# A decoder layer: the second norm's shift added in PSUM, its centring shared by VectorE, TensorE, ScalarE and GpSimd

## What is computed

```python
x = layernorm(x + self_attention(x))
x = layernorm(x + cross_attention(x, ctx))
# feed-forward part
h = gelu(silu(bitlinear158(x, w1, b1)))          # 256 -> 1024
h = (h - mean(h)) * rsqrt(var(h) + eps) * ln_g + ln_b   # "the second norm"
y = bitlinear158(h, w2, b2)                      # 1024 -> 256
x = layernorm(x + y)

def bitlinear158(x, w, b):      # 8-bit numbers times weights of -1, 0, 1
    r = x * rsqrt(mean(x * x) + eps)
    scale = 127 / max(abs(r))
    return (round(r * scale) / scale) @ quantised(w).T + b
```

## Time and profile before

| | us |
|---|---|
| median of 3 runs (lowest, highest) | 528.34 (527.87, 529.71) |
| the profiled execution | 528.22 |
| its span in the trace | 525.7 |
| busy in the span: PE / DVE / ACT / POOL | 427.8 / 439.2 / 370.2 / 294.2 |
| the tail, from its first gelu to the span's end | 421.0 to 525.7 |

### The profile page before, as it was taken

How to read it: one execution, slowest core, us unless ns; L and a number is a source line. 1 busy time by engine, 2 the same in 40 slices (tenths; PEclk the granted TensorE clock), 3 DMA queues, 4 the chain that set the end, 5 groups by cost and what they waited for, 6 DMA issues and landing times. The chain is left out here.

```text
span 525.7 us, 11922 instructions
## 1 busy us (share of the span) xinstructions
PE 427.8 (81%) x4130; PEld 231.0 (44%) x4138; DVE 439.2 (84%) x942; ACT 370.2 (70%) x690; POOL 294.2 (56%) x407
## 2 busy tenths in 40 slices
PE   6777899999999999999999999998996602555554
PEld 5453545555555555554545545443432101333332
DVE  2857697988979889799998998988877769999993
ACT  2232366778678786777877767677769878999983
POOL 6744566446474464745557455577232157667653
PEclk9998799999999999999999999999999855555557
DMA  6122313243252422424234232221000000000001
GB/s 222 50 78 65 108 42 112 67 137 113 68 153 66 138 75 65 148 56 139 76 95 144 57 109 63 68 83 52 3 2 0 1 0 1 21 21 20 32 31 40
DMA packets 52459, 37.05 MB, mean 70 GB/s; under 512 B 21552, under 2 KB 47792, under 8 KB 52400
## 3 DMA queue, kind: packets, MB, share of 16 engines
q1 hardware_dynamic: 52112, 36.06, 23.8%
q10 hardware_dynamic: 288, 0.23, 0.2%
HBM read 24.48 MB, written 10.49 MB: 67 GB/s over the span
## 5 line engine op out<-in xcount | busy, mean ns | idle before, releaser
L886 ACT ACTIVATE PB<-e_b 128x512 f32<-128x512 f32 x256 | 148.2, 592 | 59.1 <-PE e_b L683 58.0
L1080 DVE TENSOR_REDUCE MX<-mx_b 128x2 f32<-128x512 f32 x256 | 166.7, 678 | 25.3 <-PE mx_b L655 24.0
L655 PE MATMUL mx_b<-KA,QA 48*128 48x256 bf16 x512 | 98.1, 277 | 11.1 <-DVE MX L1080 10.7
L683 PE MATMUL e_b<-QA,KA 50*128 50x256 bf16 x512 | 97.3, 274 | 0.7 <-ACT PB L886 0.5
L700 PE MATMUL u_b<-PB,VA 128*32 128x256 f32 x1024 | 84.0, 391 | 2.0 <-ACT PB L886 1.7
L1007 POOL TENSOR_TENSOR SP<-SP,srec 128x1024 f32<-128x1024 f32 x15 | 28.5, 1901 | 77.7 <-DVE srec L1052 77.7
L655 PEld LDWEIGHTS mx_b<-KA,QA 48*128 48x128 bf16 x512 | 29.9, 94 | 86.0 <-issue 46.8
L1420 PE MATMUL r_b<-identh,Q 128*128 128x128 f16 x128 | 16.2, 306 | 39.4 <-ACT Q L1333 39.4
L1426 PE MATMUL z_b<-w2q,Q2T 128*128 128x256 bf16 x128 | 28.5, 400 | 19.3 <-ACT Q2T L1344 19.3
L997 POOL TENSOR_TENSOR KM<-QK,att_tab 128x512 f32<-128x512 f32 x31 | 32.0, 1053 | 21.2 <-ACT QK L840 21.2
L560 PE MATMUL g_b<-XT,wp 128*128 128x128 f32 x256 | 34.5, 291 | 4.5 <-DMA wp<-in_wpT 4.5
(11 more groups left out here) (190 smaller groups left out, 1027.2 us busy)
## 6 DMA issues: line engine op xcount, KB each, us to landing
KA<-parts_k SPq DMA_DIRECT2D x64, 96.0 KB
QA<-parts_q SPq DMA_DIRECT2D x64, 96.0 KB
parts_q<-part_q SPq DMA_DIRECT2D x32, 128.0 KB, 1.9
parts_k<-part_k SPq DMA_DIRECT2D x16, 192.0 KB, 2.1
C<-in_ctx SPq DMA_DIRECT2D x16, 128.0 KB, 3.4
X<-in_x SPq DMA_DIRECT2D x16, 128.0 KB, 2.9
out_y<-O SPq DMA_DIRECT2D x16, 128.0 KB, 1.7
XT<-in_xT SPq DMA_DIRECT2D x15, 128.0 KB, 2.2
```

The costliest lines, as they stand in the source:

```text
L655: m = nc.tensor.matmul(mx_b[n % 2][:, D * k:D * k + D], QA[low:low + K_MAX, 2 * i.ring + b, h, P * u:P * u + P], KA[low:low + K_MAX, 2 * i ...
L683: m = nc.tensor.matmul(e_b[n % 2][:, D * k:D * k + D], KA[low:low + K_EXP, 2 * i.ring + b, h, P * sc:P * sc + P], QA[low:low + K_EXP, 2 * ...
L886: nc.scalar.activation(PB[:, n % 4].rearrange("p e t -> p (e t)"), e_b[n % 2][:, :], ACT.Exp, scale=XC ** -0.5).then_inc(e_sb.sem, 1)
L1080: nc.vector.tensor_reduce(MX[:, b, e, 2 * q:2 * q + 2, u], mx_b[n % 2][:, :].rearrange("p (e s) -> p e s", e=2), AXL.X, ALU.max).then_inc( ...
```

## The change

It touches the tail and, for tables that the tail needs, three bodies of phase A.

1. Beta is added in PSUM. In bodies 10, 11 and 12 POOL splits beta into three bf16 parts (`row_parts`, ten small steps into BP, and a selector `sel`). For each pair PE writes beta with two bf16 matmuls of 512 columns, 96 rows deep, into one of three two-bank buffers `n_b` (`row_sum`), and adds the rows to it in the same buffer (`row_product`). DVE's add of beta (L1459) is gone.
2. The centring is divided. Of the columns 0 to 383 (SPLIT) DVE takes the mean off and multiplies by gamma in one instruction (`lower_columns`); the scale comes from PE, whose stationary matrix is a diagonal `DG` that holds each row's root, made by POOL. Columns 384 to 1023 go the old way, ACT (L1323) and POOL (L1371), now 640 columns wide, and PE adds them with the identity as stationary matrix. Both products are fp32. The last pair's rows are all 1024 columns of DVE's and the diagonal's.
3. The maximum (DVE), the squares and the numbers (ACT) read n_b in PSUM in place of the rows in SBUF. The numbers' and the copy's constants are immediates of a Copy (they were pointers of an Identity).
4. The additions of eps (three small DVE instructions, `base`) are one POOL instruction ahead of the power.
5. All of it has a turn less of lag from the norm on: squares at 4 (the maximum at 3), numbers at 5, result at 6; 24 turns. r_b and z_b have one buffer each. PE has a list by turns: `row_sum` of pair t-3, product of pair t-6, `row_product` of pair t-3, transposes of pair t-5.

The diff, cut:

```diff
+            def row_parts(steps):
+                for k in steps:
+                    if k > 0:
+                        pool.wait_ge(s_bp, k)
...
+                    elif k == 4:
+                        pool.wait_ge(ld_rows, 16 * 4)
+                        ins = nc.gpsimd.tensor_copy(BP[own], bet[own])
+                    elif k == 5:
+                        ins = nc.gpsimd.tensor_tensor(BR[own], bet[own], BP[own], ALU.subtract)
+                    elif k == 6:
+                        ins = nc.gpsimd.tensor_copy(BP[mid], BR[mid])
+                    elif k == 7:
+                        ins = nc.gpsimd.tensor_copy(BP[low], BR[low])
+                    elif k == 8:
+                        ins = nc.gpsimd.tensor_tensor(BR[low], BR[low], BP[low], ALU.subtract)
+                    else:
+                        ins = nc.gpsimd.tensor_copy(BP[low], BR[low])
+                    ins.then_inc(s_bp, 1)
+                pool.wait_ge(s_bp, steps.stop)
...
+                if i.v in (10, 11, 12):
+                    wait(pool, split["q"], j, 5)
+                    row_parts((range(0, 5), range(5, 8), range(8, 10))[i.v - 10])
                 if real(a):
                     self_norm(pool, nc.gpsimd, a)
...
-        r_b = [bank(f"r_b{n}", F16) for n in range(2)]
-        z_b = [bank(f"z_b{n}") for n in range(2)]
+        tail_banks.close()
+        n_b = [es.enter_context(nc.psum_tensor(f"n_b{n}", [P, INNER], F32)) for n in range(3)]
+        r_b, z_b = bank("r_b", F16), bank("z_b")
-        TURNS2 = NPAIR + 9
+        TURNS2 = NPAIR + 8
...
-        LAG_G, LAG_N, LAG_Z = 1, 5, 7
+        LAG_G, LAG_N, LAG_Z = 1, 4, 6
...
-                if i := pair_at(t, 3):
+                if i := pair_at(t, 4):
+
+                    wait(act, ymax, i, 1)
+                    if has(i, 1):
+                        wait(act, sqr, i.plus(-1), 1)
+                    nc.scalar.activation(SQ[:], n_b[i.ring][:, :], ACT.Square, scale=INNER ** -0.5,
+                                         accum_out=mom[:, t % 2, 3:4]).then_inc(sqr.sem, 1)
+                j = pair_at(t, 5)
+                if j:
+                    wait(act, fac, j, 3)
+                    if has(j, 2):
+                        wait(act, q2_ps, j.plus(-2), 1)
+                    nc.scalar.activation(Q2[:, j.p, :], n_b[j.ring][:, :], ACT.Copy, bias=ROUND16,
+                                         scale=sc[:, j.v, 6:7]).then_inc(qd.sem, 1)
+                if (i := pair_at(t, 2)) and i.v != NPAIR - 1:
                     wait(act, shift, i, 1)
-                    nc.scalar.activation(row_h(i), row_h(i), ACT.Identity, bias=nmh[:, i.p, 0:1],
+                    nc.scalar.activation(row_h(i)[:, SPLIT:], row_h(i)[:, SPLIT:], ACT.Identity, bias=nmh[:, i.p, 0:1],
                                          scale=root[:, (i.v + LAG_G) % 4, 0:1]).then_inc(zs.sem, 1)
                 if i := pair_at(t, 0):
                     wait(act, silu, i, 1)
                     nc.scalar.activation(row_h(i), row_h(i), ACT.Gelu).then_inc(gelu.sem, 1)
-                j = pair_at(t, 6)
-                if j:
-                    wait(act, fac, j, 3)
-                    if has(j, 2):
-                        wait(act, q2_ps, j.plus(-2), 1)
-                    nc.scalar.activation(Q2[:, j.p, :], row_h(j), ACT.Identity, bias=rnd16[:],
-                                         scale=sc[:, j.v, 6:7]).then_inc(qd.sem, 1)
-                if i := pair_at(t, 4):
-                    wait(act, yn, i, 1)
-                    if has(i, 1):
-                        wait(act, sqr, i.plus(-1), 1)
-                    nc.scalar.activation(SQ[:], row_h(i), ACT.Square, accum_out=sc[:, i.v, 0:1]).then_inc(sqr.sem, 1)
                 if j:
                     wait(act, q2_ps, j, 1)
                     if has(j, 2):
                         wait(act, z_ps, j.plus(-2), 1)
-                    nc.scalar.activation(Q2T[:, j.p].rearrange("p k t -> p (k t)"), r_b[j.p][:, :],
-                                         ACT.Identity, bias=nrnd16[:]).then_inc(q2_sb.sem, 1)
+                    nc.scalar.activation(Q2T[:, j.p].rearrange("p k t -> p (k t)"), r_b[:, :],
+                                         ACT.Copy, bias=-OFF16).then_inc(q2_sb.sem, 1)
 
...
+            def power(t, cols, lags):
+                if not any(pair_at(t, lag) for lag in lags):
+                    pool.sem_inc(s_root, 1)
+                    return
+                if LAG_G in lags and (i := pair_at(t, LAG_G)):
+                    wait(pool, hn, i, 3)
+                if LAG_N in lags and (i := pair_at(t, LAG_N)):
+                    wait(pool, sqr, i, 1)
+                if LAG_Z in lags and (i := pair_at(t, LAG_Z)):
+                    wait(pool, zn, i, 3)
+                nc.gpsimd.tensor_tensor(base[:, t % 2, cols], mom[:, t % 2, 1::2][:, cols], eps3[:, cols], ALU.add).then_inc(s_eps, 1)
+                powers.append(t)
+                pool.wait_ge(s_eps, len(powers))
+                nc.gpsimd.tensor_tensor(root[:, t % 4, cols], base[:, t % 2, cols], halves[:, cols], ALU.pow).then_inc(s_root, 1)
+
             def turn(t):
-                if i := pair_at(t, 4):
-
-                    wait(pool, yn, i, 1)
-                if (i := pair_at(t, 3)) and i.v != NPAIR - 1:
-                    wait(pool, zs, i, 1)
-                    nc.gpsimd.tensor_tensor(row_h(i), row_h(i), gam, ALU.mult).then_inc(zg.sem, 1)
-                if z := pair_at(t, 8):
+                if z := pair_at(t, LAG_Z + 1):
                     wait(pool, zshift, z, 1)
                     if has(z, 2):
                         pool.wait_ge(st_o[z.p], 16 * z.uses)
                     nc.gpsimd.tensor_scalar(O[:, z.p, :], Z[:, z.ring, :], root[:, (z.v + LAG_Z) % 4, 2:3], nmz[:, z.p, 0:1],
                                             ALU.mult, ALU.add).then_inc(on.sem, 1)
+                i = pair_at(t, 2)
+                if i:
+
+                    pool.wait_ge(s_root, ROOTS[t - 1])
+                    if has(i, 2):
+                        wait(pool, n_ps, i.plus(-2), 1)
+                    nc.gpsimd.tensor_scalar(DG[:, i.p, :], ident, root[:, (t - 1) % 4, 0:1], None, ALU.mult).then_inc(s_dg.sem, 1)
                 if t >= DRAIN:
-                    for col, lag in ((1, LAG_N), (2, LAG_Z)):
-                        if pair_at(t, lag):
-                            pool.wait_ge(s_base, BASES[t - 1] + 1 + (1 if col == 1 else BASES[t] - BASES[t - 1]))
...
-                elif BASES[t] > (BASES[t - 1] if t else 0):
-                    pool.wait_ge(s_base, BASES[t] + 1)
-                    nc.gpsimd.tensor_tensor(root[:, t % 4, :], base[:, t % 2, :], halves[:, 0:3], ALU.pow).then_inc(s_root, 1)
+                    power(t, slice(1, 2), (LAG_N,))
+                    power(t, slice(2, 3), (LAG_Z,))
                 else:
-                    pool.sem_inc(s_root, 1)
-
+                    power(t, slice(0, 3), (LAG_G, LAG_N, LAG_Z))
+                if i and i.v != NPAIR - 1:
+                    wait(pool, zs, i, 1)
+                    nc.gpsimd.tensor_tensor(row_h(i)[:, SPLIT:], row_h(i)[:, SPLIT:], gam[:, SPLIT:], ALU.mult).then_inc(zg.sem, 1)
...
+            def row_sum(i):
+
+                if has(i, 3):
+                    wait(pe, qd, i.plus(-3), 1)
+                for c in range(2):
+                    nc.tensor.matmul(n_b[i.ring][:, 512 * c:512 * c + 512], sel[:], BP[:, 512 * c:512 * c + 512],
+                                     start=True, stop=False)
+
+            def row_product(i):
+                wait(pe, s_low, i, 1)
+                wait(pe, s_dg, i, 1)
+                if i.v != NPAIR - 1:
+                    wait(pe, zg, i, 1)
+                low = INNER if i.v == NPAIR - 1 else SPLIT
+                for c in range(2):
+                    for stat, cols in ((DG[:, i.p, :], slice(512 * c, min(512 * c + 512, low))),
+                                       (ident, slice(max(512 * c, low), 512 * c + 512))):
+                        if cols.start < cols.stop:
+                            m = nc.tensor.matmul(n_b[i.ring][:, cols], stat, row_h(i)[:, cols], start=False,
+                                                 stop=cols.stop == 512 * c + 512)
+                m.then_inc(n_ps.sem, 1)
+
+            def numbers(j):
+                wait(pe, qd, j, 1)
+                if has(j, 1):
+                    wait(pe, q2_sb, j.plus(-1), 1)
+                for k in range(8):
+                    m = nc.tensor.transpose(r_b[:, P * k:P * k + P], low_half(Q2[:, j.p, P * k:P * k + P]), identh[:])
+                m.then_inc(q2_ps.sem, 1)
+
             def second_product(j):
-                wait(pe, qd, j, 1)
+                wait(pe, q2_sb, j, 1)
+                if has(j, 1):
+                    wait(pe, zn, j.plus(-1), 1)
                 for k in range(8):
+                    m = nc.tensor.matmul(z_b[:, 0:D], Q2T[:, j.p, k, :], w2q[:, k, :], start=k == 0, stop=k == 7)
                 m.then_inc(z_ps.sem, 1)
...
```

(91 more changed lines are left out.)

47 lines of the change are left out of this document (22 added, 25 removed).

## The result

The changed kernel takes **522.28 us**, median of 16 executions (521.39 to 527.60), the kernel before 528.53, also of 16. The ratio is 0.9891, interval 0.9874 to 0.9909: 1.1% faster, where 1.9% was forecast. The kernel is faster, as forecast, and the time lies in the range, but 4 us above the number. Four of the 16 executions took 524.5 to 527.6, with mean clocks of 0.947 to 0.957 against 0.960 to 0.964 in the others. The profiled execution took 522.18, its span is 520.1 (before 525.7).

The account below looks back on a forecast made before the run. DVE bounds the tail at 5.46 us a turn, ACT close behind. Pair 0's copy at 441.1, plus 47.1, 20.1 and 7.3, gives span 515.6; with 2.5 more 518.1, and 0.1 for the median: 518.3 us, range 515 to 531.

Parts of the forecast that it names:

- (a): Start of the tail: copy of pair 0 starts at 441.1 us in place of 442.2, 1.1 us earlier.
- (b): Steady tail, copy of pair 0 to copy of pair 10: ten turns with a gelu in each, 47.1 us.
- (c): Last turns, copy of pair 10 to pair 15: DVE's loop is the limit, 20.1 us against 22.4 before.
- (d): From the copy of pair 15 to the end: 7.3 us, against 7.4 before.
- The turn: Steady tail turn falls from 5.46 us to 4.71, set by ACT, with DVE at 4.65.
- the 0.5 of spare in that loop: Steady turn: gamma ends 0.5 us into the next turn, PE asks for it at 1.0.
- The spare in the other loop: Steady turn: DVE's maximum ends at 4.3 us, ACT asks for it at 4.71, 0.4 to spare.
- The main rival: PE's clock stays at 1.2 GHz in the tail: turns of 7.3 us, 553 us in all; chance 0.16.
- Phase A: Table steps for beta fall where POOL idles before its softmax product: charged 0, up to 0.6 us without that cover.
- The rival that waits eat half: Spare in the steady turn's two loops is used up: turn near 5.2, 523.2 us; chance 0.17 for 521 to 526.7.

Follow-up runs that it names:

- a9: Changed kernel with pointer operands put back in ACT's numbers and copy: turn 4.839 us, 100.48 us from table load to end.
- a5: Changed kernel with SPLIT 256, so 256 columns on DVE and the diagonal in place of 384: turn 4.761 us, 102.39 us from table load to end.
- a6: Changed kernel with SPLIT 512, so 512 columns on DVE and the diagonal in place of 384: turn 4.676 us, 100.75 us from table load to end.
- a8: Changed kernel with beta's two matmuls moved behind the result's product on PE: turn 4.773 us, 101.89 us from table load to end.
- a4: Changed kernel with 52 filler bf16 matmuls on PE ahead of pair 0's sum: 519.90 us, ratio 0.9815 to the kernel before.
- a1: Changed kernel with only PE's order changed, the last pair's fp32 product ahead of the result's product: one execution, 519.24 us.
- b2: Kernel before the change, with DVE's add of beta cut from 1024 columns to one: 525.39 us, ratio 0.9926.
- a7: Changed kernel with 52 filler matmuls before the tail's first fp32 product and both PE's and DVE's last-turn orders changed: 518.18 us, ratio 0.9792.
- a3: Changed kernel with last fp32 product ahead of the result's product (PE) and last norm's shift ahead of the last maximum (DVE): 520.76 us, ratio 0.9839.

## Why the prediction was right, and where it was off

The time is in the range and the direction is right. It is not where the prediction put most of its chance (515 to 521 with 0.62), but in the band of 521 to 526.7 with 0.17. Compensation helped little: three of the four terms were too small.

The profiled execution was forecast at 518.1 and took 522.18. The span is 4.5 longer than the sum, and the four terms account for it (4.4 by their rounded differences):

| step | forecast | measured | |
|---|---|---|---|
| (a) copy of pair 0 | 441.1 | 442.31 | +1.2 |
| (b) ten turns | 47.1 | 46.72 | -0.4 |
| (c) pair 10 to 15 | 20.1 | 22.84 | +2.7 |
| (d) to the end | 7.3 | 8.23 | +0.9 |

**The turn** was right: 4.67 against 4.71, ACT ahead of DVE "by a hair", as a9, a5 and a6 confirm. Its prices too: numbers 1.12, copy 1.03, centring 0.93, lower columns 0.58, maximum 1.23, gamma 1.54 (forecast 1.48). The diagonal costs 0.61, not 0.4, and the small add of eps 0.38, not 0.19, both on POOL, which has room. They made gamma later: it ends at 463.01, 0.97 after the copy's end and not 0.5, and PE's product starts at 463.16 right behind it. PE is through with the result's product at 0.93 (forecast 1.0), so the 0.5 of spare in that loop was used up, though at no cost. The spare in the other loop, 0.4, measured 0.33 (a8).

The 16 maxima from PSUM last 1.22 us on average, against 1.21 from SBUF, and DVE did not become the bound. The prediction had the right price by a circular reading: its 1.04 ns a column is the difference between a row from SBUF (1.208) and one from PSUM (0.678), and added to 0.678 it gives back 1.208 whatever the gap. The dearer start from PSUM that the Trainium skill (VectorE: DVE Perf Modes, on the TRN2 errata) gives for VectorE is not seen here, and the trace does not agree with it for these shapes.

**The clock** did not stay low in the steady turns: the granted clock is 1.00 from 450 to 495 with PE busy 12.0 to 12.7 of 15 us. The main rival fell. The Trainium skill (TensorE: Matmul & The Clock Gate, part on the PE-mode transpose) would have had the eight transposes of a turn not hold the clock; they take 0.61 of 4.67, and with the rest of the turn's work the trace does not decide about that rule. What the rival had right is that the clock costs: 1.8 at the start (a4), and 0.8 at the end, where the last product takes 1.89 in place of 1.05. The forecast had charged the low clock to the first product alone and kept 1.3 for the second as a reserve.

**(a)** It is 1.2 late: pair 0's centring starts at 425.60 and not 425.05 (0.47 of this is the load), and 0.6 more is lost before the first fp32 product. From that centring to the product the forecast counted 3.93; it took 4.55. Eps and power take 1.38 there and not 1.05, since the add lasts 0.45 beside DVE's lower columns, and gamma with its hand-over 1.69 and not 1.48. The rest was right: the product 3.75 (3.9), DVE from the first maximum to the end of the second 4.4 (4.4), ACT 3.9 (3.8). The second pair's slow sum cost nothing: its product ended at 436.63, and DVE had its lower columns to do until 437.20.

**(c)** This is the step that failed: "the loop through DVE is the limit", with hand-overs of some 4.3. The order of the lists was not walked through for the last pair. In its turn PE's product stands behind `second_product`, and POOL's power behind an output that waits for DVE behind the maximum. With PE's order mended the drain is 19.5, near the 20.1 and inside 18.5 to 22.4; 22.84 is outside. Even this nearness is in part luck: a1's first two intervals (4.51, 4.68) are longer than the 4.35 counted, and the next two (3.82, 3.75) shorter. A list of instructions that is right for steady turns need not be right for the last. PE's product of 1024 columns is no wider there than before (1.88), but the work around it is missing: DVE had nothing else to do than wait for it.

**(d)** is the clock: the last product took 1.89 in place of 1.05. The idle times of (c) go before it, but (c) alone does not decide it, since a8 and a9 had the old order and an end of 7.33 and 7.40.

**Phase A** at no charge was nearly right: POOL's softmax products start at 251.62, 273.53, 295.50, 317.44 and 339.38. The last three distances are 21.97, 21.94 and 21.94, where the kernel before has 21.91, 21.90 and 21.91, and every changed form has the same three to 0.01. The tables cost 0.13 us.

**A side remark was wrong**: "ACT's own work is 5.27. Whoever takes work from DVE alone gains 0.19 a turn". b2 gained nothing a turn. The 0.18 was read as time that DVE's work costs ACT; it is the transposes' time at 1.2 GHz, and it comes back without DVE's add. The sum did not rest on it, since it built ACT's new turn up from its parts.

The rival that waits eat half gives 523.2, nearest to the measured time, but not by its mechanism: it put the loss into the ten turns, which are shorter than forecast. The loss fell into the two ends. What it said of POOL's diagonal and gamma came true in size, at no cost to the turn.

## What to carry to other kernels

Walk a pipeline's hand-written lists through the first and the last turn by themselves: here one step's place in the last pair's turn was worth 3.3 us, nearly half of what ten steady turns gave. When an idle PE stands before a latency chain, read the granted clock of the stretch: filler matmuls ahead of it gave 1.8 us against the profiled execution of the changed kernel, and made the start the same in both forms that had them. With the gaps in the drain closed the clock held to its end in a1 and a7, not in a3. A gap on an engine is not spare until one knows what ends it, and a busy engine is not the bound until it is relieved alone (b2).
